# Expert choice moved into the first attention, attention weights loaded a stage ahead, unused products on TensorE, and a last stage gated in another way

## The reference

```python
xn = _layernorm(x)
s = L0_attn(xn)      # 16 heads of 8, window of 64 and the window before it, bias linear in the distance
g = _silu(L0_ffn(xn))  # 8 experts of 176, the best 2 by softmax, and a shared one of 352
x = x + s * g
xn = _layernorm(x)
s = L1_attn(xn)      # 16 heads of 8, all 256 keys, bias from a table of relative positions
g = _silu(L1_ffn(xn))  # two inner layers: shift_token, local attention of 8 heads of 64, gated MLP of 341
x = x + s * g
# the choice of experts in L0_ffn:
scores = softmax(xf @ gate_w.T); topw, topi = top_k(scores, 2)
topw = topw / (topw.sum(-1, keepdims=True) + 1e-20)
wdense = zeros(T, 8).at[arange(T)[:, None], topi].set(topw)
```

## Time and profile before

| | us |
|---|---|
| three runs | 1824.84, 1833.40, 1833.61; median 1833.4 |
| the profiled execution: its own time | 1827.53 |
| its span, first to last instruction | 1825.6 |
| block `front` | 0 to 50.6 |
| `window_attention` | 50.6 to about 285 |
| `experts` | about 285 to 597 |
| `normalise` | 597.1 to 606.6 |
| `bias_attention` | 606.6 to about 1010.5 |
| `inner_layers` | about 1010.6 to 1825.6 |

### The profile page before, as it was taken

One profiled execution on the slowest core, in us unless ns is written; L12 is line 12 of the kernel. 1 busy time (PEld: TensorE's weight loads), 2 busy tenths in 40 slices (PEclk: granted clock), 3 DMA queues, 4 the chain that ended last, 5 costly groups with the idle time before them and its releaser, 6 DMA issues. The chain is left out here.

```text
span 1825.6 us, 47446 instructions
## 1 busy us (share of the span) xinstructions
PE 1578.6 (86%) x18689; PEld 1181.4 (65%) x18705; DVE 1349.0 (74%) x2209; ACT 1195.5 (65%) x1987; POOL 1088.8 (60%) x637
## 2 busy tenths in 40 slices
PE   4599996999999399999999488889898889889884
PEld 4377774666666176777777267667676667777663
DVE  4599984545554499999998678787877877778753
ACT  2377774444444377777777378777777777777763
POOL 0567672454545277777776687666666666666614
PEclk9999998999999599999999589999999999999997
DMA  4100000000000500000000011111111111101111
GB/s 111 53 3 3 3 3 15 8 14 7 7 7 1 173 2 2 2 2 2 2 2 2 9 25 28 25 25 25 25 24 22 25 25 25 25 19 25 25 25 52
DMA packets 55363, 40.15 MB, mean 22 GB/s; under 512 B 27560, under 2 KB 47180, under 8 KB 55028
## 3 DMA queue, kind: packets, MB, share of 16 engines
q1 hardware_dynamic: 55156, 37.26, 8.0%
HBM read 15.66 MB, written 2.13 MB: 10 GB/s over the span
## 5 line engine op out<-in xcount | busy, mean ns | idle before, releaser
L796 POOL TENSOR_TENSOR a_prob<-a_prob,a_top 128x1024 f32<-128x1024 f32 x128 | 239.2, 1896 | 68.2 <-DVE a_top L948 68.1
L1175 POOL TENSOR_TENSOR e_hh<-e_h,e_hh 128x512 fp32r<-128x512 f32 x112 | 144.2, 1290 | 160.8 <-ACT e_hh L1159 159.3
L1694 ACT ACTIVATE i_prob<-i_prob,i_top 128x128 f32<-128x128 f32 x512 | 156.4, 391 | 38.5 <-DVE i_top L1813 36.8
L1426 POOL TENSOR_TENSOR i_qk<-i_qk,i_rn 128x1024 f32<-128x1024 f32 x64 | 123.3, 1927 | 92.0 <-DVE i_rn L1804 92.0
L923 ACT ACTIVATE a_probT<-ps 128x1024 f32<-128x1024 f32 x128 | 131.0, 1024 | 71.9 <-PE ps L852 71.8
L1413 POOL TENSOR_TENSOR i_qk<-i_raw,i_rot 128x1024 f32<-128x1024 f32 x64 | 152.0, 2376 | 28.9 <-issue 23.6
L945 DVE TENSOR_TENSOR a_prob<-ps,a_table 128x1024 f32<-128x1024 f32 x128 | 150.7, 1219 | 24.3 <-PE ps L844 15.3
L1416 POOL TENSOR_TENSOR i_qk<-i_qk,i_rt 128x1024 f32<-128x1024 f32 x64 | 151.6, 2368 | 25.0 <-DVE i_rt L1821 19.9
L1196 DVE TENSOR_TENSOR e_h<-ps,e_sg 128x512 f32<-128x512 f32 x112 | 77.2, 690 | 118.0 <-PE ps L1058 83.9
L1142 ACT ACTIVATE e_sg<-ps 128x512 f32<-128x512 f32 x112 | 67.1, 599 | 135.0 <-PE ps L1058 135.0
L948 DVE TENSOR_REDUCE a_top<-a_prob 128x4 f32<-128x1024 f32 x128 | 150.1, 1214 | 5.8
(11 more groups left out here) (276 smaller groups left out, 4378.4 us busy)
## 6 DMA issues: line engine op xcount, KB each, us to landing
i_V<-i_V SPq DMA_DIRECT2D x96, 130.0 KB, 2.3
a_table<-skew_scratch SPq DMA_DIRECT2D x2, 2048.0 KB, 12.6
X<-in_L_attn_x SPq DMA_DIRECT2D x4, 512.0 KB, 6.5
a_table<-in_c_l_table SPq DMA_DIRECT2D x1, 2048.0 KB, 7.7
e_xs<-Y SPq DMA_DIRECT2D x8, 256.0 KB, 2.3
i_ms<-Y SPq DMA_DIRECT2D x16, 128.0 KB
i_ms<-Y SPq DMA_DIRECT2D x16, 127.0 KB
out_dram<-X SPq DMA_DIRECT2D x7, 256.0 KB, 2.3
```

The costliest lines, as they stand in the source:

```text
L796: nc.gpsimd.tensor_tensor(s, s, top[:, slot].unsqueeze(2).broadcast_to([P, HG, KW]), ALU.subtract).then_inc(shifted, 1)
L1175: nc.gpsimd.tensor_tensor(hh[0:n, b % HBUF, 1, :], h[0:n, b % HBUF, :], hh[0:n, b % HBUF, 0, :].bitcast(F32), ALU.subtract).then_inc(h_lo, 1)
L1426: nc.gpsimd.tensor_tensor(flat, flat, rn[:, T // TPB % 2, T % TPB].unsqueeze(2).broadcast_to([P, 2 * FH, FD]), ALU.mult).then_inc(qk_done, 1)
L1694: last = nc.scalar.activation(s, s, ACT.Exp, bias=top[:, T % 2, h:h + 1])
```

## The change

- The choice of experts is a function `choose_experts(nc, dve, part, ...)` of six parts. Part 0 is DVE's first work in the first attention's block; parts 1 to 5 stand behind the row maxima of steps 4, 12, 20, 28 and 36. `front` ends with the exponent.
- The first attention's weights, `own` and the bias table are loaded and the weights transposed and copied in `front`. In the attention POOL clears `xT` and `kM` first and `V` last; PE and ACT no longer wait for the clears at the start (ACT waits before its first write of `V`); ACT doesn't load a table, in either attention.
- The second attention's weights and biases are issued in `normalise`, ahead of the bias table.
- `keep_busy`: four products 128x256 whose result nobody reads, in `front` ahead of the first transposes, and in the first attention at step -6.
- The shifted rows of every stage go in two transfers, of 112 and 15 rows.
- In the last part DVE makes the first inverse deviation of quad 15 itself, by a subtraction on the bits and three refinements, and ACT goes to `gelu(FINAL - 1)` at once. DVE's three copies of the value half (L1911) go; bias and gate are one instruction that reads PSUM (in place of L1971).

```diff
+def keep_busy(nc, times, out, ident, rows):
+    for _ in range(times):
+        nc.tensor.matmul(out, ident[:, :], rows.rearrange("p k e -> p (k e)"), start=True, stop=True)
@@ front, SP
             sp.dma_start(desc[:, :], t["c_descending"]).then_inc(gate_loaded, 16)
+            sp.dma_start(wnat[:, 0:3, :], t['L0_attn_w_in'].rearrange('(c p) e -> p c e', p=P)).then_inc(w_loaded, 16)
+            sp.dma_start(wnat[:, 3, :], t['L0_attn_w_out']).then_inc(w_loaded, 16)
+            sp.dma_start(attn["own"][:, :], t['c_quad']).then_inc(attn["loaded"], 16)
+            sp.dma_start(attn["table"][:], t['c_l0_table']).then_inc(attn["loaded"], 16)
@@ front, PE
             pe.wait_ge(gate_sb, 1)
+            pe.wait_ge(x_loaded[0], 16)
+            keep_busy(nc, 4, ps[:, 5, 0:2 * P], ident, X[:, 0:2, :])
...
+            pe.wait_ge(w_loaded, 32)
+            for j in range(4):
+                last = nc.tensor.transpose(ps[:, 4, j * P:(j + 1) * P], wnat[:, j, :], ident[:, :])
+            last.then_inc(w_T, 1)
             multiply(ROUNDS - 1)
@@ window_attention, PE
+                if step == FIRST + 1:
+                    keep_busy(nc, 4, ps[:, 6, 0:2 * P], ident, Y[:, 0:2, :])
@@ window_attention, DVE
+            between(dve, 0)
...
                     row_max(n + 1, (n + 1) % NBUF)
+                if step >= 4 and step % 8 == 4 and step // 8 < 5:
+                    between(dve, 1 + step // 8)
@@ normalise
-            normalise(nc, "ln1", X, Y, stats, lambda sp: load_bias_table(sp, skew, table, table_loaded))
+            normalise(nc, "ln1", X, Y, stats, lambda sp: (load_bias_weights(sp, t, attn), load_bias_table(sp, skew, table, table_loaded)))
@@ inner_layers, SP
+        SHIFTED = ((0, 112), (112, P - 1))
-                sp.dma_start(ms[1:P, :, HALF:P], Y[0:P - 1, at:at + 4, HALF:P]).then_inc(m_staged, 16)
+                for a, b in SHIFTED:
+                    sp.dma_start(ms[a + 1:b + 1, :, HALF:P], Y[a:b, at:at + 4, HALF:P]).then_inc(m_staged, 16)
@@ inner_layers, ACT
-            inverse_deviation(FINAL)
             gelu(FINAL - 1, False)
@@ inner_layers, DVE
                 if R == FINAL:
                     dve.wait_ge(qk_T, TT)
+                    nc.vector.tensor_scalar(rstd[:].bitcast(I32), var[:].bitcast(I32), -0.5, RSQRT_MAGIC, ALU.mult, ALU.add)
+                    dve.drain()
+                    for _ in range(3):
+                        nc.vector.scalar_tensor_tensor(mtmp[:], var[:], -0.5, rstd[:], ALU.mult, ALU.mult)
+                        dve.drain()
+                        nc.vector.tensor_tensor(mtmp[:], mtmp[:], rstd[:], ALU.mult)
+                        dve.drain()
+                        nc.vector.scalar_tensor_tensor(rstd[:], mtmp[:], 1.5, rstd[:], ALU.add, ALU.mult)
+                        dve.drain()
...
-            for c in range(NC):
-                keep_value(FINAL, c)
...
-                nc.vector.tensor_tensor(A[0:w, FINAL % 2, c, :], A[0:w, FINAL % 2, c, :], last_G[c][0:w], ALU.mult).then_inc(last_gated, 1)
+                nc.vector.scalar_tensor_tensor(A[0:w, FINAL % 2, c, :], ps[0:w, CHUNK_BANKS[c][1], :], b1[0:w, DEPTH - 1, 0, c:c + 1],
+                                               last_G[c][0:w], ALU.add, ALU.mult).then_inc(last_gated, 1)
```

More of the change, by code:

```diff
@@ L95, in build_kernel @@
             experts_loaded = early.enter_context(nc.semaphore("experts_loaded"))
-            front(nc, t, ps, X, Y, ident, wgu, wd, sel, experts_loaded, skew, wparts)
-            window_attention(nc, "a0", t, ps, ident, Y, S)
+            with ExitStack() as first:
+                sb = lambda n, s: first.enter_context(nc.sbuf_tensor("a0_" + n, s, F32))
+                attn = {"wT": sb("wT", [P, 4, P]), "own": sb("own", [P, 4]), "table": sb("table", [P, TPB, H, 2 * WIN]),
+                        "loaded": first.enter_context(nc.semaphore("a0_loaded"))}
+                route = router_buffers(nc, first)
+                front(nc, t, ps, X, Y, ident, wgu, wd, sel, experts_loaded, skew, attn, route)
+                window_attention(nc, "a0", t, ps, ident, Y, S, attn, lambda dve, part: choose_experts(nc, dve, part, route, wparts))
             experts(nc, t, ps, ident, X, Y, S, wparts, (wgu, wd, sel, experts_loaded), stats)
@@ L202, in front @@
+def front(nc, t, ps, X, Y, ident, wgu, wd, sel, experts_loaded, skew, attn, route):
     NR, full = ROUTED // P, SHARED // P
@@ L310, in _ @@
                 keep_transposed(i)
+            act.wait_ge(w_T, 1)
+            nc.scalar.activation(wT[:], ps[:, 4, :].rearrange("p (c e) -> p c e", c=4), ACT.Copy)
             act.wait_ge(shifted, 1)
@@ L415, in _, with window_attention @@
             dve.drain()
-def window_attention(nc, name, t, ps, ident, Y, S):
+def window_attention(nc, name, t, ps, ident, Y, S, attn, between):
     KW = 2 * WIN
@@ L434, in window_attention @@
         sem = lambda n: c.enter_context(nc.semaphore(name + '_' + n))
-        wnat = sb('wnat', [P, 4, P])
-        wT = sb('wT', [P, 4, P])
-        own = sb('own', [P, QG])
-        table = sb('table', [P, TPB, H, KW])
+        wT, own, table, b_loaded = (attn[n] for n in ('wT', 'own', 'table', 'loaded'))
         xT = sb('xT', [P, 2, PAD + SEQ])
@@ L526, in _ @@
         def _(pe):
-            pe.wait_ge(w_loaded, NWL)
-            for j in range(4):
-                last = nc.tensor.transpose(ps[:, 0, j * P:(j + 1) * P], wnat[:, j, :], ident[:, :])
-            last.then_inc(wT_ps, 1)
-            pe.wait_ge(wT_sb, 1)
-            pe.wait_ge(zeroed, NZERO)
             def job(n, kind, i):
```

185 lines of the change are left out of this document (87 added, 98 removed).

## The result

The changed kernel takes 1809.92 us at the median of 4 runs (1803.22 to 1817.57), the kernel before 1832.41 (1824.84 to 1833.61, 4 runs). The ratio is 0.9881, with a 95% interval from 0.9855 to 0.9908: 22 us faster, between 17 and 27. The forecast was 1819, its range 1799 to 1830, and its side, faster by over 0.5%, is the one that came.

The account below looks back on a forecast made before the run. PE was taken as only just the first attention's bound, with single-engine chains between blocks. Terms −16.5 + 10 − 7.3 − 1 + 3.3 = −11.5 on 1827.5 gave 1816; the middle of 1816 and 1822 gave 1819, range 1799 to 1830.

Parts of the forecast that it names:

- Front: In `front`: the choice's 13.0 us leave, the weights' transposes come in; 11.6 us less.
- the idle products: In `front` and the first attention's opening: taken as 0, range 0 to 11 us, since PE waits between rounds.
- rival (C): In `front` and opening: the idle products pay, 5 to 11 us more gain, about 1811; chance 0.10.
- Opening: First attention's start to DVE's first addition: masks follow the clears at once, 9.6 instead of 14.55 us, 5.0 less.
- Parts 1 to 5: Choice on DVE in the first attention: stalls PE, with waits for POOL instructions; 10 us more, bounds 3.4 to about 18.
- rival (D): First attention: clock halves after stalls, 4.9 us more per such cycle, slower at about 1843; chance 0.07.
- Table: From `normalise` to the second attention: weights ahead of the bias table, whose landing couldn't be read; 7.3 us less, bounds 3 to 7.5.
- Staging: Last part's input: the split frees SP's held issue, so quad 15's moments start 5.9 us sooner.
- rival (E): Shifted rows: two transfers hold SP as long as one, last part loses 9 us, about 1825; chance 0.08.
- Last part: Quad 15: nine of twelve small DVE operations each meet a POOL instruction; 3.3 us more in all.
- Rival (B): Last part: POOL and the chain miss each other, gaining up to 8 us, about 1808; chance 0.25.
- Loop and experts: Loop: SP's held issue goes, but PE bounds it and input is staged a quad ahead; 1 us less (0 to 1.5).

Follow-up runs that it names:

- nobusy_a0: The changed kernel without the four idle products in the first attention's opening; 1808.0 us, ratio 0.9864 to the kernel before.
- parts_tail: The changed kernel with part 1 of the choice behind part 0 in the opening, parts 2 to 5 behind the attention's last four divisions; 1799.6 us, ratio 0.9824.
- before_again: The kernel before, unchanged, run and profiled once more; 1832.45 us beside 1831.02, ratio 0.9999.
- split_only: The kernel before with only the shifted rows of every stage in two transfers of 112 and 15 rows; 1822.8 us, ratio 0.993.
- d_psum: The changed kernel with the running estimate of quad 15's inverse deviation kept in PSUM, one copy more; 1805.7 us, ratio 0.9868.
- best_busy: The changed kernel with ACT's inverse deviation, choice at the attention's ends, half-table wait, and one more idle product per front round; 1794.9 us, ratio 0.9775.
- d_act: The changed kernel with ACT's inverse deviation of quad 15 put back ahead of the gelu of quad 14; 1806.0 us, ratio 0.9854.

## Why the prediction came out as it did

- **Front.** The move of the choice gave 12.0 us, 11.6 predicted. The step that failed is the idle products, taken as 0 ("PE waits for DVE's rows between rounds"). That was a misreading of the kernel before, whose timeline of PE shows no idle time between rounds:

```profile
24.43 1.09 PE L268 MATMUL ps<-ident,Y 128*128 128x128 f32 x4
25.32 1.71 PE L275 MATMUL ps<-r_gwT,r_xT 128*128 128x8 f32 x8
26.88 1.09 PE L268 MATMUL ps<-ident,Y 128*128 128x128 f32 x4
```

  PE is busy from 16.02 us to the end of its rounds, at half clock all the while, and a round takes 2.45 us because PE takes that long. So a full clock could pay in every round. Rounds fell to 1.28 us while it was full, and 6.1 us were gained. My row for it, 1.09 in `front` after many products, showed what the rounds alone keep, not what a denser stretch ahead of them does. That was rival (C), with 0.10, and its 5 to 11 us hold. Idle gaps don't explain the clock here: it fell again at 23.6 us, between the rows of 0.63 and 1.09 us above, while PE was busy.
- **Opening.** 5.8 us less, 5.0 predicted, by the steps named: the masks come 5.6 us after the block's start as forecast, and from there to the addition it is 3.2 us instead of 4.1, since the first scores ran at full clock (1.12 us; 2.01 in `nobusy_a0`).
- **Parts 1 to 5.** 8.8 us more, 10 predicted. The mechanism is as forecast: part 1 takes 4.76 us instead of 2.9, the lock adds some 0.8 to each of parts 2 to 5, as in the cast above, and `parts_tail` shows that the loss is theirs. The stalls forecast were 3.6, 3.3, 1.2, 1.2 and 0.7; measured is 1.23 at part 2, so that was put 2 us too high, and the others are near. The waits make 7.2 of the 8.8 us. The rest goes with what rival (D) described, in small: in all seven profiles with parts in the middle the granted clock falls once, beside a wait of some 3.3 us, and stays low for 3.4 to 6.8 us (in the changed kernel at 74.8); in the four with the parts elsewhere it doesn't fall between 60 and 250 us. That it is the stall that makes it fall is likely, not shown; `before_again` has one such fall at 74.0.
- **Table.** 5.0 us less in this profile, up to 7.0 in the others that wait for the whole table, 7.3 predicted. What I said I couldn't read, the landing, is the 2 us between.
- **Staging.** 5.2 us less, 5.9 predicted, so rival (E) fell. In the runs the gain is larger, see `split_only`.
- **Last part.** The chain from moments to deviations took 16.4 us, 17.7 predicted, for the reason given. I left the wait of the four normalisations to the upper bound, and it came (3.83 instead of 1.11); in turn only seven of the nine operations that I counted as blocked were. So the size is in part luck: the operations ahead of the normalisations took 3.5 us less than forecast, the normalisations 2.7 more. From moments to the last products it took 31.0 us, 32.6 predicted, 21.8 before. Rival (B), that the lock spares this part, fell. The gates cost 2.05 us for the three, 2.2 predicted.
- **Loop and experts.** Predicted 1 us less in sum, measured 6.5 more in this profile, and 1.5 more in the second attention behind its first addition (387.3 in `d_psum` too, the other profile with a late table, 385.2 to 385.6 in all the rest; so a late table goes with 3.5 us in all). The code of `experts` is unchanged, that of the loop but for the staging: see the last section.
- **The sum.** The forecast's sum was 11.5 us less; the profiles differ by 9.8, because 6.5 more in front and as much less in loop and experts cancel, and the medians by 22.5. So the time fell inside the range, but the gain is twice the sum. Some 6 us of the difference are the clock in front, and the changed kernel's profile is of its slowest run. About 5 us more may lie in the split of the shifted rows, whose own runs say 9 to 17 where I had 6.9; no profile shows where.

## What to carry to other kernels

A small operation is not small if each of its kind waits for a long instruction of another engine: before moving a chain of tiny DVE operations beside GpSimd work, count those with two inputs in SBUF, and give one of the inputs a home in PSUM or run the chain first. Work that fits "anywhere" should go where its engine really waits, at the opening and the tail of a pipeline, and not into a middle where that engine has 0.2 us in hand a cycle. A stage's end should be checked for what newly comes last (here the table). And before a term is put at nothing because an engine "waits anyway", its rows at that place should show the wait.

## What the runs showed of the hardware that was not expected

Four idle products ahead of `front` raised the granted clock from 1.2 to 2.4 GHz, by its record 15 to 17 us after the start, in all ten kernels that had them; in the four without them it first rose at 45 to 80 us, though PE was busy without a gap from 16 us to the end of the rounds. In nine of the ten (all but `best_busy`) it stayed up for only 3.4 to 13.7 us, differing between profiles of the same code. The block of the attention began accordingly, between 36.1 and 28.6 us. Two windows over those rounds show it (the stretch, each engine's busy time, then the granted clock, the third number from the end):

```profile
14.00:36.00 22.00, 19.89 (x104) 18.61 (x103) 8.01 (x30) 8.92 (x19) 1.07 (x3) 0.64 0.55 170
```

```profile
14.00:29.00 15.00, 12.90 (x105) 11.40 (x103) 8.08 (x30) 8.84 (x18) 1.52 (x5) 1.00 0.77 236
```

The first is `d_act` (mean granted clock 0.64), the second `d_psum` (1.00), whose code up to there is the same. Both figures are a little high: the view counts the time ahead of the first recorded rise (16.7 and 15.6 us) as full, while the idle products there lie 0.43 us apart, against 0.21 at full clock. The added clock is thus a gain that differs by up to 7.5 us between profiles. That it widens the spread of the runs isn't shown: the changed kernel's four spread over 14 us, those of the kernel before over 9, but thirteen of its runs on another chip over 12.

The 64 steps of the loop took 769.1 to 780.5 us in fourteen profiles. Counted from 65 us into the loop, they had 8 to 12 short falls of the granted clock, each 3.4 us long by the record (the longer ones, some of 10.2 us, are left out): 769.1 us with 8, 769.4 to 776.1 with 9, 772.6 to 779.9 with 10, 776.3 to 777.1 with 11 and 779.3 to 780.5 with 12. More falls go with a longer loop, whichever kernel it was, by some 2.3 us for each. But 3.4 us at half clock lose at most 1.7 us of work, and at one count the loops still differ by up to 7 us, so the falls are not shown to be the whole cause. Often they lie 47.8 us apart, near one quad of the loop (776/16 = 48.5 us). In `experts`, three profiles without the change took 313.4 to 313.6 us and had no such fall; the eleven with it took 314.5 to 315.9 with one, 316.6 to 316.8 with two and 319.4 to 319.6 with four, about 1.5 us for each; its instructions are the same. Why the clock falls more often there stays open, and it cost the change 1 to 6 us.
